# Attention on one core: value products of two units issued together at every odd unit

## What is computed

```python
x = x + 0.5 * _L0_ffn_ref(_layernorm(x), ...)
x = x + _L0_attn_ref(_layernorm(x), ...)
x = x + 0.5 * _L0_ffn_ref(_layernorm(x), ...)
x = x + 0.5 * _L1_ffn_ref(_layernorm(x), ...)
x = x + _L1_attn_ref(_layernorm(x), ...)
x = x + 0.5 * _L1_ffn_ref(_layernorm(x), ...)
...
scores = jnp.einsum('bhqd,bhkd->bhqk', q, k) / math.sqrt(Dh)
scores = jnp.where(causal[None, None], scores + alibi[None], -jnp.inf)
weights = jax.nn.softmax(scores, axis=-1)
y = jnp.einsum('bhqk,bhkd->bhqd', weights, v)
```

## Time and profile before

| quantity | value |
|---|---|
| runs before the change | 5915.18, 5928.72, 5933.72 us |
| span of the profiled execution | 5916.1 us |
| own time of the profiled execution | not listed beside the span |
| TensorE matmul (PE) busy | 5058.1 us, 85% of the span |
| VectorE (DVE) busy | 3390.4 us, 57% |
| ScalarE (ACT) busy | 2567.7 us, 43% |
| GpSimd (POOL) busy | 1828.3 us, 31% |
| V products of the first attention | from 887.6 to 1738 us |
| V products of the second attention | from 3377.7 to 5117 us |

### The profile page before, as it was taken

How to read it: one execution, slowest core, us unless ns; L and a number is a source line. 1 busy time by engine, 2 the same in 40 slices (tenths; PEclk the granted TensorE clock), 3 DMA queues, 4 the chain that set the end, 5 groups by cost and what they waited for, 6 DMA issues and landing times. The chain is left out here.

```text
span 5916.1 us, 82750 instructions
## 1 busy us (share of the span) xinstructions
PE 5058.1 (85%) x29088; PEld 2711.9 (46%) x29088; DVE 3390.4 (57%) x6345; ACT 2567.7 (43%) x5102; POOL 1828.3 (31%) x1800
## 2 busy tenths in 40 slices
PE   6566489999978566499987999999999999799996
PEld 3455333333325455357973333333333333255896
DVE  7511468887846721241119788878888878343111
ACT  2311217776662311132215176766766766513221
POOL 2388311111101288534331122222222222104332
PEclk9778779999989687699998899999999999889998
DMA  3476561222213277606986411221221221120798
GB/s 107 116 148 149 138 171 33 62 58 68 62 53 104 76 156 151 149 26 212 330 269 198 108 37 40 63 49 40 64 47 40 64 48 40 55 69 1 267 318 268
DMA packets 503528, 659.28 MB, mean 111 GB/s; under 512 B 147310, under 2 KB 358318, under 8 KB 497998
## 3 DMA queue, kind: packets, MB, share of 16 engines
q1 hardware_dynamic: 370158, 500.99, 27.0%
q0 software_dynamic: 133056, 154.15, 13.2%
HBM read 489.33 MB, written 164.20 MB: 110 GB/s over the span
## 5 line engine op out<-in xcount | busy, mean ns | idle before, releaser
L1724 DVE TENSOR_REDUCE ea_mx<-ea_psA 128x1 f32<-128x512 f32 (+3 forms) x2304 | 1373.9, 653 | 242.0 <-PE ea_psA L1585 144.1
L1706 ACT ACTIVATE ea_pr<-ea_psB 128x512 f32<-128x512 f32 (+3 forms) x2560 | 1198.9, 535 | 567.4 <-PE ea_psB L1608 557.7
L1585 PE MATMUL ea_psA<-ex_kx,ex_qx 99*128 99x512 bf16 (+3 forms) x2560 | 868.4, 357 | 20.2 <-DVE ea_mx L1724 13.3
L1608 PE MATMUL ea_psB<-ex_qx,ex_kx 99*128 99x512 bf16 (+3 forms) x2560 | 846.2, 349 | 0.0
L1724 DVE TENSOR_REDUCE ba_mx<-ba_psA 128x1 f32<-128x512 f32 (+3 forms) x1152 | 686.2, 653 | 144.3 <-PE ba_psA L1585 95.6
L1706 ACT ACTIVATE ba_pr<-ba_psB 128x512 f32<-128x512 f32 (+3 forms) x1280 | 601.5, 536 | 288.9 <-PE ba_psB L1611 155.5
L1625 PE MATMUL ea_psO<-ea_pr,ea_vx 128*32 128x512 f32 (+3 forms) x5120 | 603.5, 543 | 20.9 <-POOL ea_pr L1554 14.0
L1585 PEld LDWEIGHTS ea_psA<-ex_kx,ex_qx 99*128 99x128 bf16 x2560 | 250.3, 98 | 551.8 <-DVE ea_mx L1724 427.8
L1585 PE MATMUL ba_psA<-bx_kx,bx_qx 108*128 108x512 bf16 (+3 forms) x1280 | 443.5, 364 | 7.8 <-PEq L1146 4.5
L1608 PE MATMUL ba_psB<-bx_qx,bx_kx 108*128 108x512 bf16 (+3 forms) x1280 | 424.9, 349 | 14.6 <-DMA bx_qx<-ba_mT 14.4
L1608 PEld LDWEIGHTS ea_psB<-ex_qx,ex_kx 99*128 99x128 bf16 x2560 | 246.5, 98 | 310.3 <-ACT ea_pr L1706 141.0
(11 more groups left out here) (528 smaller groups left out, 8260.9 us busy)
## 6 DMA issues: line engine op xcount, KB each, us to landing
de_wg<-in_L_rg SPq DMA_DIRECT2D x64, 512.0 KB, 4.7
de_wu<-in_L_ru SPq DMA_DIRECT2D x64, 512.0 KB, 5.9
de_wd<-in_L_rd SPq DMA_DIRECT2D x64, 512.0 KB, 7.3
fe_wg<-in_L_rg SPq DMA_DIRECT2D x64, 512.0 KB, 4.9
fe_wu<-in_L_ru SPq DMA_DIRECT2D x64, 512.0 KB, 5.9
fe_wd<-in_L_rd SPq DMA_DIRECT2D x64, 512.0 KB, 7.5
ae_w<-in_L_w SPq DMA_DIRECT2D x64, 384.0 KB, 3.6
ce_w<-in_L_w SPq DMA_DIRECT2D x64, 384.0 KB, 3.8
```

Source lines behind the costliest of these rows:

```text
L1585: last = nc.tensor.matmul(psA[:, slot, at:at + n], qx[0:KB, s, hh, t * P:(t + 1) * P], kx[0:KB, s, hh, k:k + n], start=True, stop=not diag)
L1608: last = nc.tensor.matmul(psB[:, slot, off:BLK], kx[0:KB, s, hh, kt * P:(kt + 1) * P], qx[0:KB, s, hh, Q * BLK + off:(Q + 1) * BLK], start ...
L1706: nc.scalar.activation(pr[:, j % 4, hh, off:BLK], psB[:, exp_slot(n), off:BLK], ACT.Exp).then_inc(s_exp, 1)
L1724: v.tensor_reduce(out, src, AX.X, ALU.max).then_inc(s_ar, 1)
```

## The change

At odd units j, and only there, V of unit j - 3 and V of unit j - 2 are issued one behind the other. V of an odd unit stays where it was; V of an even unit moves four slots later, to just ahead of its odd neighbour. Nothing else changes, and the work is the same.

```diff
@@ -1326,8 +1326,8 @@
     for n in range(NSLOT):
         j, hh = n // HV, n % HV
         order.append(("B", (j, hh)))
-        if hh == 2 and (j >= 2 or with_prev):
-            order.append(("V", j - 2))
+        if hh == 2 and j % 2 and (j >= 3 or with_prev):
+            order += [("V", j - 3), ("V", j - 2)]
         order += at.get(n, [])
     return order
```

## The result

The changed kernel takes 5949.49 us (median of seven runs, 5943.70 to 5954.50), the kernel before 5928.72 us in seven runs (5909.79 to 5933.72): a ratio of 1.0048 with a 95% interval of 1.0034 to 1.0062, while the medians alone stand 0.35% apart. **It is slower, by 0.35 to 0.5 per cent.** The profiled execution has a span of 5951.5 us and an own time of 5953.29. Its span is 35.4 us over that of before; the medians are only 20.8 apart, since the span of before lay 12.6 us under its median and this one lies 2.0 over. From the first matmul behind V of unit 1 in their first step to their last V, the two attentions take 7.9 and 28.8 us more; the rest of the program takes 1.3 less.

What follows compares the result with a forecast made beforehand. PE was taken as the bound, with DVE close behind. The terms, +21 - 3 + 7 - 11 = +14 us on the profiled span of 5916.1, gave 5943 us against the median 5928.7; range 5880 to 5990.

Steps and rivals of the forecast that it cites:

- within 0.3%: Whole kernel: 5943 us, +0.24%, too little to tell from no change; likeliest case, chance 0.42, own range 5911 to 5947.
- regular and first steps, second attention: Second attention: each step 1.4 us longer, over 15 steps, +21 us.
- regular and first steps, first attention: First attention: each step 0.5 us shorter, over 7 steps, -3 us.
- last steps: Last step of each attention: B waits for ACT's exponents, +0.77 us per affected stretch, together about +7 us.
- waits for GpSimd, units 16 to 21: PE's waits ahead of V for late masks, mostly at unit 20: about -11 us, bounded by 0 and -14.
- The pair's saving: Two V in a row on PE: 0.24 us saved per pair, 115 us for 478 pairs if PE remains the bound.
- the ring's price: Three banks for A: waiting for DVE's reduces makes a stretch of two full units 0.30 us longer instead of 0.24 shorter.
- The clock I leave at 1.00: PE's granted clock: stays at 1.00, since waits of some 0.2 us each leave PE over 90% busy.
- GpSimd's masks slow the small DVE operations: First two stretches of a step, at DVE's levels: 10.0 us if masks slow DVE, otherwise 9.7, against 9.32 before.
- the ring does not bind, or less (1 and 2): Three banks for A hold nothing up, 5814 us, chance 0.07; or hold up less, about 5880 us, chance 0.13.
- binds harder through the load (3): Last A of a stretch: its weight load behind the wait costs 0.11 us per bound stretch, 5972 us; chance 0.35.
- Unhidden weights (4): Second V: each of its two passes waits 0.11 us for weights, 0.22 per pair, 6048 us at most; chance 0.03.

Runs made afterwards that it cites:

- the single V at the start: Changed kernel with V of units -2, -1, 0 and 1 each back in its old place: 5928.13 us, 1.0021 to the kernel before.
- half reduces: VectorE reads only every second column of each maxima bank, in the changed kernel and in the kernel before: 5788.21 and 5898.24 us, one run each.

## Why the prediction was right, and where it was wrong

**The time** lay in the range (5880 to 5990; forecast 5943, measured 5949). **The case did not**: I gave the largest chance to "within 0.3%", and it came out slower (ratio 1.0048), the side that had 0.38. In the terms of the sum, from the two profiles (14 regular steps of the second attention, 6 of the first):

| term | forecast, us | measured, us |
|---|---|---|
| regular and first steps, second attention | +21 | 14 x 1.55 + 2.4 = +24.1 |
| regular and first steps, first attention | -3 | -1.1 |
| last steps | +7 | +11.9 |
| waits for GpSimd, units 16 to 21 | -11 | -16.7 |
| clock in stretches 0/1 and 2/3 | 0 | +10.5 |
| sign product beside a mask | 0 | +4.4 |
| transfers awaited in the first attention | 0 | +3.4 |
| sum | +14 | +36.5 |

The step's 1.55 us is made of its twenty stretches, each by its median in the second attention; the first stretch is put at the 5.68 us it has at full clock, stretch 10/11 at 4.29, and 20/21 at its shortest (4.96 and 5.03). What they took beyond that, with what stretch 2/3 took beyond 3.97, are the rows on the clock and the sign product. The waits for GpSimd are taken from the stretches of units 16 to 21, where they fall. The last steps are counted from V of unit 39 of the step before to their last V. The transfers differ from one execution to the next.

**Part of the agreement in time is luck.** The misses add up to 22.5 us between the two profiles. The medians, to which the forecast was tied, stand only 20.8 us apart, and so 5943 comes near 5949.

**The pair's saving and the ring's price were right.** Forecast 3.56 us to the eighth A and 5.95 for stretch 14/15, measured 3.57 and 5.96; 5.45 for 32/33, measured 5.44; 6.23 for 34/35, measured 6.24; 4.71 for a stretch of the last step, and its V stand 4.72 to 4.73 apart (below). The seven longer stretches of a step, in the order of the forecast, took 0.30, 0.39, 0.17, 0.32, 0.13, 0.42 and 0.12 us more.

```profile
5131.18 1.92 PE L1625 MATMUL ea_psO<-ea_pr,ea_vx 128*32 128x512 f32 x16
...
5135.90 1.92 PE L1625 MATMUL ea_psO<-ea_pr,ea_vx 128*32 128x512 f32 x16
...
5140.63 1.92 PE L1625 MATMUL ea_psO<-ea_pr,ea_vx 128*32 128x512 f32 x16
```

The two stretches that the forecast takes together at +0.5 are 38/39 and 0/1; where the clock holds they are +0.33 (3.97 + 5.68 against 9.32).

The last steps were counted too low. In the first attention four stretches took about the forecast price (0.79 us), but five beside them took 0.43 to 0.54 each; in the second three took 0.79, and three more 0.79 to 0.86.

**The step that failed is "The clock I leave at 1.00 ... the waits that come are some 0.2 us each, which leaves PE over 90% busy".** I had counted the wait for the levels in the same text ("now both V come behind the wait") and priced it as time only. It is 1.04 us in one piece and 0.34 soon after, PE is busy 2.5 of 4 us there, and the windows then show the clock at 0.57 to 0.58 in a place where before it stood at 1.00. It costs 10.5 us, and the single V at the start brought the clock back. Why it falls in seven steps and not in seven others with the same waits, these traces do not tell.

The trace of before had such falls already. Three of its eight waits at unit 20 were 2.51 to 3.83 us long, and the clock fell behind each; here is V of unit 20 behind the longest, with the windows around it:

```profile
3865.75 1.94 PE L1625 MATMUL ea_psO<-ea_pr,ea_vx 128*32 128x512 f32 x8 [3.83 <-POOL ea_pr L1554]
3864.00:3866.00 2.00, 0.25 (x4) 0.23 (x8) 0.00 (x0) 0.00 (x0) 1.99 (x4) 0.70 0.05 6
3866.00:3868.00 2.00, 2.00 (x10) 0.28 (x3) 0.00 (x0) 0.00 (x0) 0.19 (x1) 0.50 0.04 8
```

This V took 1.94 us instead of 1.07. The three stretches were 16.1 us over their shortest for 8.9 us of waiting, so some 7 us were the clock's; the five shorter waits cost only 0.07 us each beyond their length. The change took these 7 us away with the waits, and so this term could pass the bound of -14 that the forecast had given it.

**The second miss is smaller.** I had foreseen that "GpSimd's masks slow the small DVE operations", but at the levels, not at K, whose sign product met a mask in most steps of the changed kernel.

**The rivals.** That the ring does not bind, or less (1 and 2), falls with the 5.96 us of stretch 14/15. That it binds harder through the load (3) falls too: the load waits with its A (0.48 us at 4207.34) and the A starts 0.01 us behind it, at the forecast time; the kernel was slower, as this rival has it, but by another cause. Unhidden weights (4) fall with the 0.24 us that sixteen of twenty stretches gained under half reduces. By the rule of the Trainium skill, "TensorE: Matmul & The Clock Gate", Part 3, The mechanism, that a weight load overlaps a running matmul only across different row groups, the second V should have paid for its loads; these runs speak against it here, since all four tiles use the full 128 rows and the second V still cost 0.85 us (1.92 less 1.07), its columns alone. The same section of the Trainium skill also lets a load into the background weight buffer go ahead of running matmuls; whether that is what happens here, no run shows.

## What to carry to other kernels

Grouping work that an engine is slow to switch into saves a fixed price per group, but it also bunches the work of its neighbour: count, stretch by stretch, whether the buffers between the two hold one bunch, and group only where they do. Here the same idea lost 0.5% when it was applied everywhere; in chosen places the kernel was 0.8% faster, with about two thirds of that in the attentions. When work is moved behind a wait that it used to fill, look at the wait's length in one piece and at the clock that follows, not only at the time lost in it.

## What the hardware showed that I had not expected

- The fall of the granted clock above: after 4 us with PE busy 2.5, V took 2.79 us in place of 1.71, and only in some steps.
- VectorE and GpSimd, VectorE's sign product first, then GpSimd's mask beside it, in a step of the changed kernel where they collide:

```profile
4081.70 0.73 DVE L1754 TENSOR_SCALAR ea_sm<-ea_sm,e_sgn 128x64 f32<-128x64 f32 x1
...
4081.74 0.64 POOL L1554 TENSOR_SCALAR_AFFINE_SELECT ea_pr<-ea_pr 128x512 f32<-128x512 f32 x1 [0.47 <-ACT ea_pr L1706]
```

The product ends at 4082.43, 0.05 us behind the mask (4082.38). In an earlier step it starts at 3635.54 and the mask 0.08 us behind it, at 3635.62; there it takes 0.25 us. So 0.04 us more or less decide over 0.48. The Trainium skill, "SBUF — State Buffer", Who interferes with whom, says that such an operation of VectorE can need the port pair it shares with GpSimd, and that whoever comes first holds it for a whole instruction while the other stands still. The rows agree with the standing still; by the starts alone the product was 0.04 us ahead and yet waited.
